# Distances inside the experts' groups, and an alignment that runs in two column halves

## The chip, the cores and the metric

The kernel runs on one core of a Trainium2 chip. The metric is device time in microseconds (us), the median of several runs. The core has five engines that run their own instruction streams and wait for each other by semaphores: PE (TensorE, matmuls), DVE (VectorE), ACT (ScalarE), POOL (GpSimd) and SP (SyncE, which issues the DMAs here).

## What is computed

Sixty-four sequences of 128 tokens, 256 wide, go through four residual steps. Cut to its core the reference is:

```python
x = x + xattn(ctx, layernorm(x), ...)            # attention, 16 heads
x = x + moe_ffn(layernorm(x), ...)               # 16 experts, 4 chosen, and a shared one
x = x + align(ctx, layernorm(x))                 # below
x = x + bit_ffn(layernorm(x), w1, conv, w2)      # ternary weights, depthwise convolution

def align_one(small, large):                     # small = ctx[b], large = layernorm(x)[b]
    aa = sum(small * small, -1)[:, None]; bb = sum(large * large, -1)[None, :]
    D = sqrt(maximum(aa + bb - 2.0 * small @ large.T, 0.0))
    # R[i,j] = D[i,j] + min(R[i-1,j], R[i,j-1], R[i-1,j-1]), then the path is traced back
    # from the corner, and small[i] is added to row j for each (i, j) on the path
```

## The kernel before

The program is a row of stages, each in a block of its own with a barrier at its end: `attention`, `experts`, `distances`, `align`, `conv_ffn`. `x_all` holds all tokens in SBUF throughout. Within a stage every engine has a program written out by hand; the order in it is the order of execution, and semaphores carry the dependences.

`attention` works on pairs of sequences. `norm_a`, `norm_b`, `norm_c` on DVE measure mean and variance of the tokens and of the context and normalise them.

`experts` works on 16 groups of four sequences (GB = 4, NG = 16). A group has per = 12 tiles t = 0 to 11 of hidden units: four shared, then eight routed (TILES = 8). For tile n = 12 g + t, PE does `up_gate(n)` (L838) and then `down_proj(n - 2)` (L876); ACT takes the silu (`gate_silu`, L937) and the high part (`high_hidden`, L943); DVE does `weigh_hidden(n)` (L1067 and L1072), POOL the low part (`low_hidden`, L1120). The next group's input is made in the same loop: DVE normalises at t = 1, PE turns it at t = 5 and 6 (`turn`, L815) and makes the router's scores at t = 7 (L824), and DVE chooses the experts in five steps at t = 8, 9, 10, 11 and 0 (`route_groups` ends at L1032, `route_mask` at L1040, then `route_compare`, `route_rank`, `route_weights`). PE turns the weights at t = 1 (L831), they go by DRAM (`shares`), and SP loads them spread over partitions into `spread`, one slot for each of the eight routed tiles.

`distances` makes D for groups of four sequences in a stage of its own. It loads `ctx` and its transposed copy `ctxT`, measures and normalises x a third time (DVE L1259, L1262, L1271; POOL L1312, L1313), turns it (PE L1197), multiplies it by -2 (`copy_x`, DVE L1281), squares it (ACT L1229), sums the context's squares (ACT L1237), multiplies (PE L1212 with a matrix of ones, L1214 with `ctxT`), adds and clamps (DVE L1290), takes the root (ACT L1246) and stores to `dist` in DRAM.

`align` loads `dist` to SBUF with 64 sequences on half of the partitions: even rows of D on partitions 0 to 63, odd ones on 64 to 127. DVE makes one row after another: a minimum of the row above with itself shifted (L1533), then a scan along the 128 columns (L1534). So each instruction works on 64 partitions. Each 16 rows (a chunk), `compare` writes flags (L1503, L1504), PE swaps them between the halves (L1445, L1448), `trace` makes a start column for every cell (L1511 and the scan L1517), PE and ACT turn that to `rise` (L1459, L1460, L1475). Then 128 dependent steps trace the path back (L1548). ACT and PE also make the ternary weights of the last stage in here (`sum_up` L1382, `make_ternary` L1393 to L1396).

Of the kernel before, what the change touches and what calls it, by code (L numbers as in the profile page):

```python
# [14 lines left out]
P = 128  # L15
# [8 lines left out]
EPS = 1e-5  # L24
# [47 lines left out]
def attention(nc, dve_step, pool_step, x_all, ident, half, x, ctx, wq, wkv, wo, ln_cols):  # L72
# [16 lines left out]
    with Stage(nc, "attention") as st:  # L89
# [7 lines left out]
        mv = [st.sb(f"mean_var{i}", [P, 4, 2]) for i in range(2)]  # L97
        var_eps = [st.sb(f"var_eps{i}", [P, 4]) for i in range(2)]
# [393 lines left out]
        def dve_program(dve):  # L492
# [196 lines left out]
def experts(nc, dve_step, pool_step, x_all, ident, half, router, bias, gate, up, down, s_gate, s_up, s_down, shares):  # L689
    TILES = ROUTED // P  # L690
    STILES = SHARED // P
    STAGES = 3
    with Stage(nc, "experts") as st:
# [14 lines left out]
        spread = st.sb("spread", [P, TILES, GB * TOK])  # L708
        stage = [spread[:, TILES - 2 * i - 2:TILES - 2 * i, :].rearrange("p m t -> p (m t)") for i in range(STAGES)]
        combT = st.sb("combine_turned", [EXPERTS, GB * TOK])  # L710
# [17 lines left out]
        wsum = st.sb("weight_sum", [P, 2, GB])  # L728
        misc = st.bank("misc")
        g_ps = [st.bank(f"gate{i}") for i in range(2)]  # L730
# [10 lines left out]
        spread_loaded = [st.sem(f"spread_loaded{m}") for m in range(TILES)]  # L741
# [3 lines left out]
        down_made, out_added = st.sems("down_made", "out_added")  # L745

# [34 lines left out]

        def is_routed(n):
            return n % per >= STILES

        def sp_program(sp):
            sp.dma_start(router_w[:, :, :], router.rearrange("(k p) n -> p k n", p=P)).then_inc(small_loaded, 16)
            sp.dma_start(bias_w[:, :], bias).then_inc(small_loaded, 16)
            for n, (src, buf, hi, lo) in enumerate(staged):
                if n >= STAGES:
                    sp.wait_ge(w_split, n - STAGES + 1)  # L790
                sp.dma_start(buf, src).then_inc(stage_loaded[n % STAGES], 16)
            for g in range(NG):
# [3 lines left out]
                for m in range(TILES):  # L796
                    if g:
                        sp.wait_ge(silu_weighed, TILES * (g - 1) + m + 1)
                    elif m == TILES - 2 * STAGES:
                        sp.wait_ge(w_split, R_DOWN)  # L800
                    for e in range(2):
                        sp.dma_start(spread[e * HID:(e + 1) * HID, m, :],
                                     shares[g % 2, 2 * m + e:2 * m + e + 1, :].broadcast_to([HID, GB * TOK])
                                     ).then_inc(spread_loaded[m], 16)

        def pe_program(pe):
# [74 lines left out]

            for k in range(KD):
                turn(0, k)
            route_scores(0)
            for n in range(N + 2):
                g, t = divmod(n, per)
                if n < N:
# [5 lines left out]
                if g + 1 < NG:  # L893
                    if t in (5, 6):
                        turn(g + 1, t - 5)
                    if t == 7:
                        route_scores(g + 1)

        def act_program(act):
# [5 lines left out]
            def copy_x(g, k):  # L905
                act.wait_ge(turned, 2 * g + k + 1)
                if g and not k:
                    act.wait_ge(logits_made, g)
                    act.wait_ge(xT_split, g)
                act.copy(xT[:, k, :], misc[:, :]).then_inc(xT_copied, 1)  # L910
# [15 lines left out]
            def copy_weights(g):  # L926
                act.wait_ge(comb_turned, g + 1)
                if g:
                    act.wait_ge(shares_stored, 16 * g)
                act.copy(combT[:, :], misc[0:EXPERTS, :]).then_inc(comb_ready, 1)  # L930
# [38 lines left out]
        def dve_program(dve):  # L969
# [11 lines left out]
            def norm(g):  # L981
# [6 lines left out]
                if g:  # L988
                    dve.wait_ge(turned, 2 * g)
                dve.wait_ge(rstd_made, g + 1)  # L990
# [70 lines left out]
            def weigh_hidden(n):  # L1061
                s = n % 2
                dve.wait_ge(silu_made, n + 1)
                if is_routed(n):
                    g, m = divmod(spreads(n), TILES)
                    dve.wait_ge(spread_loaded[m], 32 * (g + 1))
# [7 lines left out]
            def add_out(g):  # L1074
# [4 lines left out]
                made.then_inc(out_added, 1)  # L1079

# [7 lines left out]
            for n in range(N + 2):  # L1088
# [10 lines left out]
                if n >= 8 and (n - 8) % per < 5 and (n - 8) // per + 1 < NG:  # L1099
                    route[(n - 8) % per]((n - 8) // per + 1)  # L1100

        def pool_program(pool):
# [19 lines left out]

            inverse_std(0)
            low_x(0)
            for n in range(N):
                g, t = divmod(n, per)
                low_hidden(n)
                if g + 1 < NG:
# [4 lines left out]

        with nc.Block() as block:
            block.sync(sp_program)
            block.tensor(pe_program)
            block.scalar(act_program)
            block.vector(dve_program)
            block.gpsimd(pool_program)

def distances(nc, dve_step, pool_step, x_all, ident, half, ctx, ctxT, dist):
    with Stage(nc, "distance") as st:
# [1057 lines left out]
```

## Time and profile before

| | us |
|---|---|
| median of 3 runs | 3542.32 (3541.22 to 3543.53) |
| the profiled execution | 3543.53 |
| its span in the trace | 3541.8 |
| attention, until | 1841 |
| experts, until | 2739.7 |
| distances, until | 2837 |
| align, until | 3057 |
| conv_ffn, until | 3541.8 |

PE is busy 89% of the span, DVE 69%, ACT 52%, POOL 38%. These are means over stages with different limits, so they are read by stage: a windows view gives for a stretch how long each engine was busy, and which clock TensorE was granted (1.00 is 2.4 GHz, 0.50 is 1.2 GHz). A timeline view gives single instructions with start and duration; "[2.65 <-DVE ...]" behind one is how long its engine had been idle and what ended that.

### The profile page before, as it was taken

What the parts mean: (1) busy time and instruction counts of PE and PEld (TensorE: products, weight loads), DVE (VectorE), ACT (ScalarE), POOL (GpSimd) and SP (SyncE); (2) the same over time, 40 slices, a digit from 0 to 9 for tenths busy, and PEclk for the clock granted to TensorE, in tenths of its full rate; (3) what the DMA queues carried; (4) which work ended last, traced back from release to release, by engine and by line L of the source; (5) the groups of instructions that cost most, each with busy time, mean ns of one, the idle gap of its engine ahead of it and who ended that gap; (6) DMA issues with size and microseconds to landing.
All of it is one profiled execution on the core that took longest, in us unless ns stands there. A gap on an engine that the chain in (4) does not pass through costs nothing. (4 is left out here: it accounts for less than half of the span.)

```text
span 3541.8 us, 63842 instructions
## 1 busy us (share of the span) xinstructions
PE 3136.5 (89%) x23236; PEld 2706.4 (76%) x23236; DVE 2437.3 (69%) x5376; ACT 1838.3 (52%) x4701; POOL 1345.0 (38%) x1112
## 2 busy tenths in 40 slices
PE   7999999999999999999978999999999811177876
PEld 6888888888888888888877888888888800155655
DVE  6666666666666666666646656566564989689997
ACT  5565565555556555555633333333332602299996
POOL 2333333333333333333322333333333200078887
PEclk9999999999999999999989999999999955598888
DMA  4000000000000000000011011110111740001100
GB/s 152 5 7 7 5 7 5 7 7 4 8 4 7 4 7 8 4 7 4 5 37 59 33 49 32 42 49 25 49 49 35 225 86 0 12 31 37 42 30 31
DMA packets 104181, 107.96 MB, mean 30 GB/s; under 512 B 7872, under 2 KB 85184, under 8 KB 103872
## 3 DMA queue, kind: packets, MB, share of 16 engines
q1 hardware_dynamic: 103872, 103.88, 9.9%
q8 instruction: 189, 3.10, 0.4%
q14 instruction: 120, 0.98, 0.1%
HBM read 90.75 MB, written 13.11 MB: 29 GB/s over the span
## 5 line engine op out<-in xcount | busy, mean ns | idle before, releaser
L671 POOL TENSOR_TENSOR attention_prob<-attention_prob,attention_inv_sums 128x1024 f32<-128x1024 f32 x256 | 479.6, 1894 | 410.1 <-DVE attention_inv_sums L565 410.1
L442 ACT ACTIVATE attention_prob<-attention_turns,attention_neg_max 128x256 f32<-128x256 f32 x1024 | 468.7, 483 | 174.6 <-DVE attention_neg_max L556 174.6
L1120 POOL TENSOR_TENSOR experts_hidden_lo<-experts_weighed,experts_hidden_hi 128x512 fp32r<-128x512 f32 x192 | 251.8, 1312 | 552.2 <-ACT experts_hidden_hi L943 552.2
L572 DVE COPY attention_probT<-attention_turns 128x512 f32<-128x512 f32 x512 | 329.1, 685 | 169.2 <-PE attention_turns L329 169.1
L556 DVE TENSOR_REDUCE attention_neg_max<-attention_turns 128x2 f32<-128x512 f32 x512 | 318.1, 684 | 45.3 <-PE attention_turns L319 44.4
L943 ACT ACTIVATE experts_hidden_hi<-experts_weighed 128x512 fp32r<-128x512 f32 x192 | 121.4, 632 | 423.6 <-DVE experts_weighed L1072 423.6
L433 ACT COPY attention_v<-attention_turns 128x512 f32<-128x512 f32 x256 | 151.0, 590 | 316.5 <-PE attention_turns L263 316.5
L329 PEld LDWEIGHTS attention_turns<-ident,attention_prob 128*128 128x128 f32 x2048 | 240.2, 141 | 39.7 <-POOL attention_prob L671 4.2
L329 PE MATMUL attention_turns<-ident,attention_prob 128*128 128x128 f32 x2048 | 266.1, 273 | 3.7 <-POOL attention_prob L671 3.7
L1067 DVE TENSOR_TENSOR experts_silu<-experts_silu,experts_spread 128x512 f32<-128x512 f32 x128 | 89.3, 698 | 260.6 <-ACT experts_silu L937 259.5
L345 PE MATMUL attention_heads_out<-attention_probT,attention_v 128*64 128x128 f32 x4096 | 253.7, 277 | 0.8 <-DVE attention_probT L572 0.8
L345 PEld LDWEIGHTS attention_heads_out<-attention_probT,attention_v 128*64 128x64 f32 x4096 | 222.7, 137 | 18.2 <-DVE attention_probT L572 1.2
L660 POOL TENSOR_TENSOR attention_kv_lo<-attention_kv_full,attention_kv_hi 128x256 fp32r<-128x256 f32 x124 | 90.4, 729 | 375.0 <-ACT attention_kv_hi L411 375.0
L565 DVE RECIPROCAL attention_inv_sums<-attention_row_sums 128x4 f32<-128x4 f32 x256 | 44.8, 175 | 268.1 <-ACT attention_prob L442 268.1
L442 ACT ACTIVATION_READ_ACCUMULATOR attention_prob<-attention_turns,attention_neg_max 128x1 f32 x1024 | 220.5, 215 | 0.0
L407 ACT ACTIVATE attention_kv_full<-attention_turns,attention_ln_cols 128x128 f32<-128x128 f32 x256 | 102.3, 449 | 225.8 <-PE attention_turns L256 225.8
L876 PE MATMUL experts_out<-experts_down_hi,experts_hidden_hi 128*128 128x256 f32 x768 | 217.6, 283 | 0.4 <-POOL experts_hidden_lo L1120 0.4
L876 PE MATMUL experts_out<-experts_down_hi,experts_hidden_lo 128*128 128x256 f32 x768 | 217.2, 283 | 0.0
L876 PE MATMUL experts_out<-experts_down_lo,experts_hidden_hi 128*128 128x256 f32 x768 | 216.9, 282 | 0.0
L263 PE MATMUL attention_turns<-attention_wkv_hi,attention_kv_hi 128*128 128x512 f32 x512 | 213.6, 417 | 2.1 <-DVE attention_kv_lo L590 2.1
L295 PE MATMUL attention_turns<-attention_kv_hi,attention_wkv_hi 128*128 128x512 f32 x512 | 214.7, 419 | 0.0
L538 DVE SCALAR_TENSOR_TENSOR attention_k_lo<-attention_turns,attention_k_hi 128x512 fp32r<-128x512 f32 x256 | 177.1, 692 | 47.3 <-ACT attention_k_hi L425 41.3
(266 smaller groups left out, 9823.2 us busy)
## 6 DMA issues: line engine op xcount, KB each, us to landing
experts_spread<-shares SPq DMA_DIRECT2D x256, 128.0 KB, 3.0
attention_ctx<-in_ctx SPq DMA_DIRECT2D x32, 256.0 KB, 2.7
distance_ctx<-in_ctx SPq DMA_DIRECT2D x16, 512.0 KB, 4.4
distance_ctxT<-in_ctxT SPq DMA_DIRECT2D x32, 256.0 KB, 5.0
weights_ctx<-in_ctx SPq DMA_DIRECT2D x16, 512.0 KB, 4.0
out<-conv_x_out SPq DMA_DIRECT2D x15, 512.0 KB, 3.0
x_all<-in_x SPq DMA_DIRECT2D x7, 1024.0 KB, 9.3
dist<-distance_dist SPq DMA_DIRECT2D x16, 256.0 KB, 2.4
```

Source lines behind the costliest of these rows:

```text
L263: made = pe.matmul(out, left[l](k), right[r](k), start=n == 0, stop=n == 3 * KD - 1)
L295: made = pe.matmul(bank[:, :].rearrange("p (e c t) -> p c e t", e=2, c=2), wkv_p[l][:, k, w:w + P], (kv_hi, kv_lo)[r][p % 2][:, k, :, :, : ...
L329: made = pe.transpose(bank[:, (2 * h + t) * P:(2 * h + t + 1) * P], prob[n % 2][:, 2 * g + h, t * P:(t + 1) * P], ident[:, :])
L345: made = pe.matmul(heads_out[o * HEAD:(o + 1) * HEAD, (QT * e + m) * TOK:(QT * e + m + 1) * TOK], v[:, home, e, t, h, :], probT[e][:, h, t ...
L433: act.copy(v[:, 0:2 + pj % 2:1 + pj % 2, e, t, :, :].rearrange("p q h c -> p q (h c)"), bank_of("v", c)[:, :].rearrange("p (q c) -> p q c" ...
L442: made = act.activation(prob[n % 2][:, h, :], bank_of("s", 2 * n + e)[:, m * 256:(m + 1) * 256], ACT.Exp, bias=neg_max[:, n % 2, 2 * e + m ...
L538: return dve.scalar_tensor_tensor(lo, view, scale, hi.bitcast(F32), ALU.mult, ALU.subtract)
L556: made = dve.tensor_reduce(neg_max[:, n % 2, 2 * e:2 * e + 2], bank_of("s", 2 * n + e)[:, :].rearrange("p (h c) -> p h c", h=2), AX.X, ALU ...
L572: dve.tensor_copy(probT[n % 2][:, 2 * g:2 * g + 2].rearrange("p h t c -> p (h t c)"), bank_of("t", 2 * n + g)[:, :]).then_inc(p_copied, 1)
L671: pool.tensor_tensor(prob[n % 2][:, :, :], prob[n % 2][:, :, :], inv[:, n % 2, :].unsqueeze(2).broadcast_to([P, QH, 2 * TOK]), ALU.mult).t ...
L876: made = pe.matmul(out_ps[i // 2][:, (i % 2) * DIM:(i % 2 + 1) * DIM], l[n % 3][:, i * TOK:(i + 1) * TOK], down_w[r][:, m, :], start=t == ...
L1120: pool.tensor_tensor(hid_lo[n % 3][:, :], weighed[n % 2], hid_hi[n % 3][:, :].bitcast(F32), ALU.subtract).then_inc(hid_split, 1)
```

## The change

The stage `distances` is gone. What it did is spread over the program:

- In `attention`, `norm_c` gets two more DVE instructions for each pair of sequences, each on 128x2 numbers: from mean and variance they make the context's sum of squares in `ctx_norm`.
- In `experts`, the distances of group g are made while group g + 1 is worked on ("far"). DVE measures at t = 2, normalises at t = 7, copies the turned halves times -2 at t = 8 and 9, clamps at t = 11. POOL makes the inverse deviation at t = 2 and, at t = 9, squares both halves (L1261 twice) and adds them (L1266). PE turns one half at t = 8 and one at t = 9 (L931), both ahead of that tile's `up_gate`, and multiplies at t = 11 ahead of `up_gate` (L942 with a matrix of 0.25, L944 twice, for each of four sequences: 12 matmuls where there were 16). The last group follows behind the loop. The squared distance is stored, without the root.
- `spread` has six slots in place of eight, used as a ring, and the tile `far` shares its first partitions with the weights on their way to DRAM.
- In `align`, D is cut by columns: partitions 0 to 63 have columns 0 to 63 of all rows, partitions 64 to 127 have columns 64 to 127, two rows behind (LAG = 2). One DVE instruction makes row t of the left half and row t - 2 of the right half, 128 partitions by 64 or 65 columns, in 130 steps in place of 128. D is loaded in four parts of 8, 24, 32 and 64 rows, each in two DMAs, in pieces of 64 numbers (256 bytes) where a piece was a row of 512 bytes. ACT carries the left half's last number of each row to the right half (`hand_over`), and takes the roots of eight rows at a time (`root`). PE gathers both flags of a chunk by 16 matmuls in place of 4, ACT copies one of them. The ternary weights are made in single ACT steps between the rows. The trace back is as it was.

The core of the diff:

```diff
@@ attention, norm_c
+                mean, var = mv[0][:, 2:4, 0], mv[0][:, 2:4, 1]
+                dve_step(dve, dve.scalar_tensor_tensor(mean_part[:, :], mean, float(DIM), mean, ALU.mult, ALU.mult))
+                dve.scalar_tensor_tensor(ctx_norm[:, 2 * p:2 * p + 2], var, float(DIM), mean_part[:, :], ALU.mult,
+                                         ALU.add)
@@ experts, PE
+            def turn_far(g, k):
+                pe.wait_ge(far_normed, g + 1)
+                if k:
+                    pe.wait_ge(far_copied, 2 * g + 1)
...
+            def multiply(g):
+                pe.wait_ge(ctx_loaded, 32 * (g + 1))
+                pe.wait_ge(far_copied, 2 * g + 2)
+                pe.wait_ge(far_summed, g + 1)
...
                 g, t = divmod(n, per)
+                for k in range(KD):
+                    if far_in(n, 8 + k) is not None:
+                        turn_far(far_in(n, 8 + k), k)
+                if far_in(n, 11) is not None:
+                    multiply(far_in(n, 11))
                 if n < N:
                     up_gate(n)
@@ experts, DVE, at the end of a tile's work
+                if far_in(n, 2) is not None:
+                    measure_far(far_in(n, 2))
+                if far_in(n, 7) is not None:
+                    norm_far(far_in(n, 7))
+                for k in range(KD):
+                    if far_in(n, 8 + k) is not None:
+                        copy_far(far_in(n, 8 + k), k)
+                if far_in(n, 11) is not None:
+                    clamp(far_in(n, 11))
@@ align, loads
-            rows = dist.rearrange("b (s h) j -> b s h j", h=2)
-            for c in range(LOADS):
+            for c, (a, b) in enumerate(LOADS):
                 for h in range(2):
-                    sp.dma_start(cost[lanes[h], 1 + c * LR:1 + (c + 1) * LR, 1:], rows[:, c * LR:(c + 1) * LR, h, :]
+                    sp.dma_start(cost[lanes[h], 1 + h * LAG + a:1 + h * LAG + b, 1:], dist[:, a:b, h * W:(h + 1) * W]
@@ align, ACT
+            root(0)
+            for t in range(N):
+                hand_over(t)
+                if t % PIECE == 3:
+                    root(t // PIECE + 1)
```

What this moves, at the places of which the next sections speak. On DVE in `experts`, from the last two instructions of `route_groups` (t = 8) to the weighing of tile 9. Before:

```order
L1031 TENSOR_TENSOR experts_tops<-experts_tops 128x16
L1032 TENSOR_TENSOR experts_group_score<-experts_tops 128x16
L1067 TENSOR_TENSOR experts_silu1<-experts_silu1,experts_spread 128x512
L1072 TENSOR_TENSOR experts_weighed<-experts_silu1,experts_up1 128x512
L1000 TENSOR_TENSOR experts_group_compare<-experts_group_score 128x16
```

After (`experts_far_ps` is the PSUM bank that holds the turned half):

```order
L1111 TENSOR_TENSOR experts_tops<-experts_tops 128x16
L1112 TENSOR_TENSOR experts_group_score<-experts_tops 128x16
L1187 TENSOR_SCALAR experts_xT<-experts_far_ps 128x512
L1147 TENSOR_TENSOR experts_silu1<-experts_silu1,experts_spread 128x512
L1152 TENSOR_TENSOR experts_weighed<-experts_silu1,experts_up1 128x512
L1080 TENSOR_TENSOR experts_group_compare<-experts_group_score 128x16
```

The copy L1187 of the first turned half stands behind the whole of `route_groups`; the second stands in the same way behind `route_mask`, a tile later.

On POOL, around t = 9 of a group, after (before, the five `experts_hidden_lo` rows follow each other directly):

```order
L1249 TENSOR_TENSOR experts_hidden_lo0<-experts_weighed,experts_hidden_hi0 128x512 [waits experts_hidden_high]
L1261 TENSOR_TENSOR experts_xn<-experts_xT 128x512 [waits experts_far_copied,experts_far_turned]
L1261 TENSOR_TENSOR experts_xn<-experts_xT 128x512 [waits experts_far_copied]
L1266 TENSOR_TENSOR experts_far<-experts_xn 128x512 [waits experts_shares_stored,experts_far_stored,experts_far_squared]
L1249 TENSOR_TENSOR experts_hidden_lo1<-experts_weighed,experts_hidden_hi1 128x512 [waits experts_hidden_high]
```

Three more instructions stand between the low parts of tiles 9 and 10, and PE's `multiply` waits for the last of them.

## Rows read from the trace of the kernel before

**Rows 1.** Windows: us, busy time and count by engine, then clock, DMA share, GB/s.

```profile
1936.00:2740.00 804.00, 799.51 (x4692) 701.66 (x4689) 489.16 (x1157) 254.74 (x428) 285.55 (x222) 1.00 0.13 41
2739.70:2837.00 97.30, 78.68 (x640) 75.25 (x640) 83.72 (x289) 60.96 (x177) 20.46 (x34) 0.93 0.76 217
```

**Rows 2.** Timeline, PE, first matmul of `up_gate` at t = 5 and 7.

```profile
2111.03 0.39 PE L838 MATMUL experts_gate<-experts_xT_hi,experts_gate_hi 128*128 128x512 f32 x1
...
2120.23 0.48 PE L838 MATMUL experts_gate<-experts_xT_hi,experts_gate_hi 128*128 128x512 f32 x1
```

**Rows 3.** Timeline, PE, first matmul of `up_gate` at t = 9 and 11.

```profile
2130.54 0.40 PE L838 MATMUL experts_gate<-experts_xT_hi,experts_gate_hi 128*128 128x512 f32 x1
...
2138.99 0.39 PE L838 MATMUL experts_gate<-experts_xT_hi,experts_gate_hi 128*128 128x512 f32 x1
```

**Rows 4.** Timeline, DVE: last instruction of `route_groups` (t = 8), of `route_mask` (t = 9).

```profile
2132.47 0.17 DVE L1032 TENSOR_TENSOR experts_group_score<-experts_tops 128x16 f32<-128x16 f32 x1
...
2137.76 0.22 DVE L1040 TENSOR_TENSOR experts_masked<-experts_masked,experts_group_neg 128x64 f32<-128x64 f32 x1
```

**Rows 5.** Timeline, POOL, the low part of tile 9.

```profile
2135.02 1.31 POOL L1120 TENSOR_TENSOR experts_hidden_lo<-experts_weighed,experts_hidden_hi 128x512 fp32r<-128x512 f32 x1 [2.92 <-ACT experts_hidden_hi L943]
```

**Rows 6.** Lines by form, DVE in `distances`: count, busy us, mean ns, idle before.

```profile
L1281 DVE TENSOR_SCALAR distance_xT<-distance_turned 128x512 f32<-128x512 f32 x32 | 20.4, 679 | 0.0
...
L1290 DVE TENSOR_SCALAR distance_squared_dist<-distance_dist_ps,distance_ctx_norm 128x128 f32<-128x128 f32 x64 | 17.6, 338 | 7.2 <-PE distance_dist_ps L1214 7.2
```

**Rows 7.** Timeline of `distances`: DVE's first normalising, and two matmul groups on PE.

```profile
2743.32 1.38 DVE L1271 TENSOR_SCALAR distance_xn<-x_all,distance_mean_var,distance_rstd 128x256 f32<-128x256 f32 x4 [1.47 <-POOL distance_rstd L1313]
...
2757.61 0.61 PE L1212 MATMUL distance_dist_ps<-distance_xT_square,distance_ones 128*128 128x128 f32 x4
...
2758.50 0.61 PE L1212 MATMUL distance_dist_ps<-distance_xT_square,distance_ones 128*128 128x128 f32 x4
```

**Rows 8.** Timeline, PE in `conv_ffn`: what follows a wait of 2 to 3 us.

```profile
3112.67 0.63 PE L1732 MATMUL conv_hidden_turned<-ident,conv_act_h 128*128 128x128 f32 x4 [2.65 <-DVE conv_h_absmax_part L2005]
...
3141.63 0.63 PE L1732 MATMUL conv_hidden_turned<-ident,conv_act_h 128*128 128x128 f32 x4 [1.97 <-DVE conv_h_absmax_part L2005]
...
3499.36 0.96 PE L1732 MATMUL conv_hidden_turned<-ident,conv_act_h 128*128 128x128 f32 x4 [2.46 <-DVE conv_h_absmax_part L2005]
```

**Rows 9.** Windows, columns as in rows 1: after the first of these waits.

```profile
3113.90:3117.30 3.40, 3.40 (x12) 2.71 (x11) 2.77 (x8) 3.40 (x9) 1.09 (x1) 0.51 0.00 0
```

**Rows 10.** Lines by form, DVE, columns as in rows 6.

```profile
L1534 DVE TENSOR_TENSOR_SCAN align_cost<-align_best,align_cost 64x128 f32<-64x128 f32 x128 | 53.6, 419 | 12.0 <-DMA align_cost<-dist 7.6
...
L1533 DVE TENSOR_TENSOR align_best<-align_cost 64x128 f32<-64x128 f32 x127 | 36.3, 286 | 4.3
...
L1517 DVE TENSOR_TENSOR_SCAN align_back<-align_left,align_moved 128x1024 bf16<-128x1024 bf16 x8 | 18.3, 2292 | 0.3
...
L1504 DVE TENSOR_TENSOR align_left<-align_cost,align_best 128x1024 bf16<-128x1024 f32 x8 | 9.7, 1218 | 0.0
...
L1052 DVE TENSOR_TENSOR experts_combine<-experts_score,experts_rank 128x64 f32<-128x64 f32 x2 | 0.5, 226 | 0.1
```

**Rows 11.** Windows: while `dist` is loaded, and while `ctx` and weights are.

```profile
2840.00:2845.00 5.00, 0.00 (x0) 0.00 (x0) 0.00 (x0) 0.00 (x0) 0.00 (x0) 0.50 1.24 190
...
2862.00:2865.00 3.00, 0.00 (x0) 0.00 (x0) 2.76 (x8) 0.00 (x0) 0.00 (x0) 0.50 1.04 380
```

**Rows 12.** Timeline: SP's loads of `dist`, DVE's first row, its last `trace`.

```profile
2836.96 16.24 SPq L1434 DMA_DIRECT2D align_cost<-dist  x8
...
2845.20 0.42 DVE L1534 TENSOR_TENSOR_SCAN align_cost<-align_best,align_cost 64x128 f32<-64x128 f32 x1 [7.56 <-DMA align_cost<-dist]
...
2990.75 2.29 DVE L1517 TENSOR_TENSOR_SCAN align_back<-align_left,align_moved 128x1024 bf16<-128x1024 bf16 x1
```

More of the change, by code:

```diff
@@ L780, in spreads, with far_in @@
             return g * TILES + max(0, t - STILES)
+        def far_in(n, tile):
+            g, t = divmod(n, per)
+            return g - 1 if t == tile and 0 < g < NG else None
         def is_routed(n):
@@ L897, in pe_program @@
                         route_scores(g + 1)
+            for k in range(KD):
+                turn_far(NG - 1, k)
+            multiply(NG - 1)
         def act_program(act):
@@ L1100, in dve_program @@
                     route[(n - 8) % per]((n - 8) // per + 1)
+                if far_in(n, 2) is not None:
+                    measure_far(far_in(n, 2))
+                if far_in(n, 7) is not None:
+                    norm_far(far_in(n, 7))
+                for k in range(KD):
+                    if far_in(n, 8 + k) is not None:
+                        copy_far(far_in(n, 8 + k), k)
+                if far_in(n, 11) is not None:
+                    clamp(far_in(n, 11))
+            measure_far(NG - 1)
+            norm_far(NG - 1)
+            for k in range(KD):
+                copy_far(NG - 1, k)
+            clamp(NG - 1)
         def pool_program(pool):
@@ L1377, in means, with sum_up @@
         dve.reciprocal(self.inv[:, :], self.mean[:, :]).then_inc(self.inverted, 1)
[L1379 to L1387 removed]
+    def sum_up(self, act, n):
+        if not n:
+            act.wait_ge(self.loaded, 96)
+        made = act.activation(self.junk[:, :], self.raw[:, n, :], ACT.Abs, accum_out=self.sums[:, n:n + 1])
+        if n:
+            made.then_inc(self.summed, 1)
+        else:
+            self.act_step(act, made)
@@ L1479, in act_program, with hand_over, root @@
-            for c in range(CHUNKS):
-                rises(c)
-                if c == 2:
-                    weights.sum_up(act)
-                if c == 5:
-                    weights.make_ternary(act, 0)
-                if c == 6:
-                    weights.make_ternary(act, 1)
+            def hand_over(t):
+                act.wait_ge(row_made, t + 1)
+                act.copy(best[lanes[1], place(t + LAG), 0:1], cost[lanes[0], t + 1, W:W + 1]).then_inc(handed, 1)
+            def root(p):
+                for c, (a, b) in enumerate(LOADS):
+                    if PIECE * p == a:
+                        act.wait_ge(loaded[c], 32)
+                a = 1 + PIECE * p
+                b = min(a + PIECE, SLOTS)
+                if not p:
+                    act.activation(cost[lanes[0], a:b, 1:], cost[lanes[0], a:b, 1:], ACT.Sqrt)
+                    made = act.activation(cost[lanes[1], a + LAG:b, 1:], cost[lanes[1], a + LAG:b, 1:], ACT.Sqrt)
+                elif PIECE * p < N:
+                    made = act.activation(cost[:, a:b, 1:], cost[:, a:b, 1:], ACT.Sqrt)
+                else:
+                    made = act.activation(cost[lanes[1], a:b, 1:], cost[lanes[1], a:b, 1:], ACT.Sqrt)
+                made.then_inc(rooted, 1)
@@ L1488, in pool_program @@
+            rises(CHUNKS - 2, 0)
+            for b in range(2):
+                copy_left(CHUNKS - 1, b)
+            for b in reversed(range(2)):
+                rises(CHUNKS - 1, b)
         def pool_program(pool):
```

505 lines of the change are left out of this document (240 added, 265 removed).

## The prediction, made before the changed kernel ran

> **What bounds the kernel now.** I read the windows by stage first, then the timeline of each engine over one group of `experts`, then the stages `distances` and `align`. In `experts` PE is busy 799.51 of 804.00 us at clock 1.00, DVE 489 and POOL 286 [rows 1]: every instruction that PE gets here, and every wait, lengthens the program, while DVE and POOL have room on the mean. `distances` lasts 97.3 us with no engine full [rows 1]. In `align` DVE is a chain of dependent instructions on 64 partitions: from its first row at 2845.20 to the end of the last `trace` scan at 2990.75 + 2.29 = 2993.04 are 147.8 us [rows 12].
>
> **The stage that goes.** −97.3 us. Its last group stays, behind the loop, as a chain with nothing beside it. In the old stage the first normalising begins 3.6 us after the start at 2739.70 and takes 1.4 us [rows 1, 7]. Then come two turns and two copies (1.1 us each at the lower clock, an estimate from twice the rate in rows 2, and 0.68 us [rows 6]), 3.6; POOL's second square and its sum, 2 x 1.31 [rows 5], 2.8 with the handovers; the multiplication, which at clock 1.00 costs 0.89 us for 8 matmul records [rows 7], so 2.7 us for 24 (12 fp32 matmuls, two records each) and 5.4 us at the lower clock; the clamps, 4 x 0.29 = 1.2 (mean 0.338, overlapping [rows 6]); a store and the barrier, 3 us. Together 21 us (bounds 16 and 26). Net **−76**.
>
> **PE's new work in a group.** From the `up_gate` of t = 5 to that of t = 7 are 9.20 us with two turns between [rows 2], from t = 9 to t = 11 8.45 us without [rows 3]: 0.75 for two turns. Multiplying costs 2.7 us and 0.1 for the switch. Together 3.5 us, nothing hides it. PE idles 4.5 us in all 15 groups [rows 1], mostly where it waits for the combine weights; that goes: −0.3. So **+3.2** a group.
>
> **The first new wait.** PE's turn of the second half stands ahead of `up_gate` at t = 9 and waits for `copy_far(g, 0)`, since both halves use one bank. That copy stands on DVE behind all of `route_groups`, which ends at 2132.47 + 0.17 = 2132.64 [rows 4]. With the copy (0.06 + 0.68 us [rows 6]) it is done at 2133.40, while PE is through with t = 8 at 2130.54 [rows 3]. Both sides shift alike with the turn at t = 8. PE waits **2.9 us**, and all of PE's queue with it.
>
> **The second.** `multiply` stands ahead of `up_gate` at t = 11 and waits for POOL's sum. The chain from t = 9: `route_mask` ends at 2137.76 + 0.22 = 2137.98 [rows 4], `copy_far(g, 1)` at 2138.72, the second square (1.31 [rows 5]; the first is done by then) and the sum at 2141.5 with 0.1 for each handover. PE is there at 2138.99 [rows 3]. PE waits **2.6 us**. The two waits add up, because everything between them hangs on PE's own results. DVE's clamp (1.2 us at t = 11) delays the routing weights by less than PE has been delayed (6 to 9 us), so it costs nothing; if PE did not wait, it would cost at most that 1.2 us.
>
> Sum: 3.2 + 2.9 + 2.6 = 8.7 us in each of 14 groups, 122 us. In the last one nothing is routed: 3.5 us of work, and waits of 0.2 and 1.3 us by the same reckoning without the routing steps, 5 us. **+127**. `measure_far` and `norm_far` (1.8 and 1.4 us at t = 2 and 7) fall where DVE has time; POOL's three instructions at t = 9 (3.9 us) delay the low part of tile 10, which PE wants two tiles later; SP's store and two loads stand between its loads of `spread`, in a stage with a DMA share of 0.13 [rows 1]. At nothing, with 0 to 15 us as the bound if the store (aliased with the weights' tile) comes late by up to 1 us a group.
>
> **TensorE's clock.** Each wait also puts the clock at stake. In `conv_ffn` a wait of 2.65 us was followed by 3.4 us at 0.51, and one of 2.46 us by slow transposes (0.96 against 0.63 us); after one of 1.97 us they were fast [rows 8, 9]. 3.4 us at half clock cost PE 1.7 us of work. The wait of 2.9 us is longer than those that were punished; that of 2.6 us is beside them, but PE has been full before it, which it is not in `conv_ffn`. I take one fall a group: 14 x 1.7 = **+24**; bounds are none, 0, and a fall of twice that length after both, 14 x 6.6 = 92.
>
> **Alignment.** A row now is a minimum of 64 columns and a scan of 65. The minimum: 286 ns at 128 columns, 226 ns for a 128x64 instruction of the same kind [rows 10]. The scan: 419 ns at 128 columns, 2292 ns at 1024 [rows 10], so 2.09 ns a column and 288 ns at 65 (bounds 250 and 350). With the same 70 ns of handovers as now, 0.584 us in place of 0.775; 130 steps are 75.9 where 128 were 99.2: −23.3. The chunks cost DVE the same: three instructions of 1.22 and a scan of 2.29 [rows 10] against two, one more and the same scan; 0. Against that:
> - At the end the last `trace` waits for 16 matmuls at the lower clock, a quarter the size of 1024 columns in 4: estimated 3.8 us (2 to 5).
> - ACT carries one number to the right half for each row. DVE has 0.88 us between a row's end and the scan that needs it, and the copy costs some 0.23 with 0.17 of handovers, so it hides, also behind one root or copy of 0.6 us; the 2 us steps of the weights stand where DVE is in `compare` or `trace` (3.7 and 2.3 us). I take +0.7; if ACT is late each time, 10 x 1.2 = 12.
> - The loads. 512-byte pieces arrive at 190 GB/s, larger ones at 380 [rows 11]: 2.7 and at least 2.7 ns a piece, so pieces and not bytes set the rate. 256-byte pieces then need 44 us for the 4.2 MB. The second part (rows 8 to 31) is there 13.8 us after the start, its first root at 14.5. DVE begins at 7.9 (loads, a table load, two roots; 8.2 now [rows 12]), is at row 6 at 11.4 and must wait there, since ACT, which waits for the load inside `root(1)`, carries nothing: +3.4, and +1.3 when ACT waits in the same way for the weights, queued behind D. Bounds 0 and 10.
>
> −0.3 − 23.3 + 3.8 + 0.7 + 4.7 = **−14.4** (−24 to 0).
>
> By the Trainium skill, "DMA: Bandwidth & Descriptors", section "Why small descriptors are slow (HBM only)", a packet has a fixed cost of some three cycles, 11 for 256 bytes, so that halving it would cost little: D would be there in an estimated 26 us and the 3.4 us would go. The same page's "Specifications" put the line rate at 512 bytes and more. Rows 11 speak for a price per piece.
>
> **Attention.** 64 DVE instructions, 0.2 us each, before `add_out`, which waits for PE there: 0 (bound 3).
>
> **Sum**, on the profiled execution's 3543.5 us: −76 + 127 + 24 − 14.4 + 0 = +60.6, 3604.1. That execution is 1.2 us above the median: **3603**.
>
> **Rivals.**
> - *The clock never falls.* The waits stand, PE's full stretches carry the clock over them. 3603 − 24 = 3579.
> - *The clock falls after both waits, for long.* 3603 + 68 = 3671; with the short fall after both, 3627.
> - *Faster: the waits don't come.* The mechanism is that DVE runs ahead in t = 8 and 9, or PE's matmuls in `up_gate` end later by the records than I read them, so that both copies are ready when PE is. The first wait is gone from the point where `route_groups` ends 0.8 us (the copy) before PE is through with t = 8, at 2129.8, which is 2.9 us earlier than its 2132.64 now [rows 3, 4]. Then `experts` gains only 3.2 x 14 + 3.5 + 1.2 x 2 = 51 us, and the sum is −76 + 51 − 14 = −39: 3503. The order on DVE speaks against it.
> - *The alignment gives nothing*, by late carrying or loads: 3603 + 14 = 3617.
> - *The work does not leave the path at all* is what the first sum says already; the opposite, that moved work hides, needs PE to have room, and it has 4.5 us of 804.
>
> **Chances.** Forecast with one fall, or some, a group (3590 to 3648): 0.50. No fall: 0.22. Long falls: 0.10. Alignment nothing beside the forecast: 0.05, within its range. Waits absent or so small that the kernel is faster: 0.13. The range takes in the no-fall case with a gain of 24 in the alignment and a tail of 16, 3579 − 10 − 5 = 3564, and short falls after both with the alignment's gain lost and half of the store's bound, 3627 + 14 + 7 = 3648; outside are the faster case and most of the long falls. A measurement of this kernel tells about 0.2% (7 us) from no change; faster 0.13, same 0.03, slower 0.84.
>
> **What would show it.** In the changed profile: a group of `experts` takes 63 us or more, not 54; PE's L931 of the second half waits some 2.9 us for DVE's L1187, its L942 some 2.6 us for POOL's L1266; the granted clock of the stage is below 1.00; the tail between the last add and `align` is 21 us; a row of `align` 0.58 us with one halt of 3 us near row 6. If PE's waits there are below 1 us, the prediction is wrong by its largest term; if the clock is 1.00, by its third.

## The result

The changed kernel takes 3646.9 us (median of 4 runs, 3645.7 to 3650.5) against 3542.1 before (4 runs): a ratio of 1.0297, 95% interval 1.0279 to 1.0315, so 105 us slower. 3603 was predicted, with a range of 3564 to 3648: the direction and the mechanism held, the size was 44 us short.

The traces of the two profiled executions are split here at the same events: the last add of `attention`, the end of the last add of `experts`, the first load of `align`, the end of the trace back.

| | before, us | after, us | difference | predicted |
|---|---|---|---|---|
| attention, to its last add | 1840.9 | 1848.4 | +7.5 | 0 |
| experts | 898.8 | 1100.3 | +201.5 | +151 |
| distances; after: the last group's | 97.3 | 20.1 | −77.2 | −76 |
| align | 219.1 | 194.7 | −24.4 | −14.4 |
| the rest | 485.7 | 485.1 | −0.6 | 0 |
| span | 3541.8 | 3648.6 | +106.8 | +60.6 |

Windows of the changed kernel: one over the same stretch of `experts` as [rows 1], then two right behind PE's two new waits in one group. The columns are those of [rows 1].

```profile
1936.00:2740.00 804.00, 727.91 (x4126) 643.65 (x4125) 501.96 (x1178) 208.52 (x347) 292.89 (x240) 0.94 0.14 43
2793.92:2797.32 3.40, 3.40 (x11) 2.90 (x12) 0.00 (x0) 0.00 (x0) 0.00 (x0) 0.56 0.00 0
2807.86:2812.86 5.00, 5.00 (x23) 5.00 (x24) 3.22 (x7) 0.00 (x0) 1.26 (x1) 0.50 0.00 0
```

In the same 804 us PE is busy 728 us where it was busy 799.5 [rows 1], and its granted clock is 0.94 where it was 1.00. Behind the two waits of this group it is 0.56 and 0.50, at or near the 1.2 GHz level. Over the 14 groups of this execution it falls behind the first wait in 11 and behind the second in 14. The waits themselves, in the view of waits of `experts` (us in total, times, longest), and two stores of `dist`, one group apart:

```profile
PE experts_far_ps L942 <- POOL experts_far L1266: 53.8, 16, 3.6
PE experts_far_ps L931 <- DVE experts_xT L1187: 40.2, 15, 3.1
...
2822.84 0.37 SPq L822 DMA_DIRECT2D dist<-experts_far  x1
...
2891.11 0.37 SPq L822 DMA_DIRECT2D dist<-experts_far  x1
```

Between these two stores a group takes 68.3 us, where it took 54.1; the 14 groups take 951.3 us together, 68.0 each, because the groups in which the first wait left the clock alone are 1.0 to 2.6 us shorter. These are the two waits that were forecast, on the lines that were forecast. In one group they read so on PE, with the instructions of the first chain on DVE and of the second on DVE and POOL:

```profile
2789.80 0.69 DVE L1152 TENSOR_TENSOR experts_weighed<-experts_silu,experts_up 128x512 f32<-128x512 f32 x1
...
2792.88 0.17 DVE L1112 TENSOR_TENSOR experts_group_score<-experts_tops 128x16 f32<-128x16 f32 x1
2793.09 0.69 DVE L1187 TENSOR_SCALAR experts_xT<-experts_far_ps 128x512 f32<-128x512 f32 x1
...
2793.92 1.09 PE L931 MATMUL experts_far_ps<-ident,experts_xn 128*128 128x128 f32 x4 [2.78 <-DVE experts_xT L1187]
...
2800.22 2.39 DVE L1086 TENSOR_TENSOR experts_group_compare<-experts_group_compare,experts_below 128x16 f32<-128x16 f32 x4
2800.24 1.30 POOL L1249 TENSOR_TENSOR experts_hidden_lo<-experts_weighed,experts_hidden_hi 128x512 fp32r<-128x512 f32 x1 [7.72 <-ACT experts_hidden_hi L1021]
...
2801.51 1.06 POOL L1261 TENSOR_TENSOR experts_xn<-experts_xT 128x512 f32<-128x512 f32 x1
...
2804.09 0.69 DVE L1187 TENSOR_SCALAR experts_xT<-experts_far_ps 128x512 f32<-128x512 f32 x1
...
2804.86 1.42 POOL L1261 TENSOR_TENSOR experts_xn<-experts_xT 128x512 f32<-128x512 f32 x1 [2.28 <-DVE experts_xT L1187]
2806.35 1.36 POOL L1266 TENSOR_TENSOR experts_far<-experts_xn 128x512 f32<-128x512 f32 x1
...
2807.86 0.77 PE L942 MATMUL experts_far_ps<-experts_far,experts_quarters 128*128 128x128 f32 x2 [3.51 <-POOL experts_far L1266]
```

From start to start of `up_gate`, tile by tile, this group loses against the one before the change: 0.5 us at t = 7 to 8 (a turn), 3.7 at t = 8 to 9 (wait 2.8, turn 0.9), 1.1 at t = 9 to 10 (nothing but the lower clock), 8.8 at t = 10 to 11 (wait 3.5, multiplication 5.3) and 0.5 behind it (clock); 0.4 is won at the combine weights. Together 14.2.

### The profile page after: what moved, and what is told of

It reads as the page before. It is cut to its first block and busy times, and to the rows that moved or that the text cites. A ratio compares the mean times of both kernels' runs of the same rounds, so it can differ in the third digit from the quotient of the medians.

```text
span 3648.6 us, 64032 instructions
## 1 busy us (share of the span) xinstructions
PE 3193.5 (88%) x23204; PEld 2757.7 (76%) x23204; DVE 2461.4 (67%) x5446; ACT 1823.0 (50%) x4687; POOL 1405.7 (39%) x1164
## 5 line engine op out<-in xcount | busy, mean ns | idle before, releaser
L1015 ACT ACTIVATE experts_silu<-experts_gate 128x512 f32<-128x512 f32 x192 | 114.2, 595 | 351.4 <-PE experts_gate L879 351.4
```

## Experiments: the two waits and the clock

Theory A: PE pays for its new work, for two waits, and for the half clock behind them. The rivals are that the clock falls for another reason, and that a wait taken away turns up elsewhere. Three kernels form a square with the change: both waits, one, the other, none. A fourth keeps both but leaves PE almost no idle time.

**Both waits away.** On DVE the copies go ahead of the routing step; on POOL the first square goes ahead of the low part of tile 9.

```diff
+                for k in range(KD):
+                    if far_in(n, 8 + k) is not None:
+                        copy_far(far_in(n, 8 + k), k)
                 if n >= 8 and (n - 8) % per < 5 and (n - 8) // per + 1 < NG:
                     route[(n - 8) % per]((n - 8) // per + 1)
...
-                for k in range(KD):
-                    if far_in(n, 8 + k) is not None:
-                        copy_far(far_in(n, 8 + k), k)
...
+                if far_in(n, 9) is not None:
+                    square_far(far_in(n, 9), 0)
                 low_hidden(n)
```

> The changed kernel with one move on DVE: at t = 8 and 9 the copy of the turned half stands ahead of the routing step, not behind it; on POOL the square of the first half stands ahead of the low part of tile 9. Theory A (PE lost 2.8 and 3.5 us a group to two waits, and 4.3 us to the half clock behind them): both waits fall below 0.5 us, the clock of the stage is 1.00, a group takes 57.7 us instead of 68.3, the kernel 3647 - 14 x 10.6 = 3499 us. Theory B (the waits go but the clock still falls, since something else than the waits makes it fall): 3647 - 14 x 6.3 = 3559. Theory C (the copies ahead of the routing make the routing weights late, the waits only move): 3620 to 3650.

Measured: 3527.8 us, 119 less than the change and 15 less than the kernel before (0.9963, 0.9950 to 0.9975). Waits and windows of `experts`:

```profile
PE experts_misc L872 <- DVE experts_combine L1136: 14.2, 14, 1.0
...
PE experts_far_ps L942 <- POOL experts_far L1268: 4.8, 6, 3.6
...
1950.00:2800.00 850.00, 831.03 (x4988) 730.29 (x4987) 607.70 (x1397) 248.04 (x417) 345.55 (x286) 1.00 0.17 51
```

Both waits are gone (3.6 of the 4.8 us are the last group's, behind the loop) and the clock is 1.00. B, that the clock falls without the waits, is excluded. A small part of C is true: PE now waits 1.0 us in each of 14 groups for the combine weights, which DVE makes later, with the clamp ahead of them. Most groups take 59.0 to 59.3 us, not 57.7, and the change's took 68.0 on the mean, not 68.3; by these two the kernel is at 3528 and not at the 3499 that A gave.

**Only the first wait away.**

```diff
+                if far_in(n, 8) is not None:
+                    copy_far(far_in(n, 8), 0)
                 if n >= 8 and (n - 8) % per < 5 and (n - 8) // per + 1 < NG:
...
-                for k in range(KD):
-                    if far_in(n, 8 + k) is not None:
-                        copy_far(far_in(n, 8 + k), k)
+                if far_in(n, 9) is not None:
+                    copy_far(far_in(n, 9), 1)
```

> The changed kernel, only the copy of the first half (t = 8) moved ahead of the routing step; the second stays behind it. Theory A: the first wait (2.8 us) and its half clock (0.4 us in the turn, 1.1 us in up_gate) go, the second wait of 3.5 us stays because its chain starts at tile 9's own results: 3647 - 14 x 4.3 = 3587 us. Theory D (the two waits hang on one chain on DVE, so that what the first gives the second takes): the second wait grows to 6 us, 3647.

Measured: 3574.0 us. The second wait stays at 3.5 us, so D, that it grows by what the first gives, is excluded; but 73 us are won, not 60. The wait, and windows at its end, in two groups:

```profile
2487.24 0.76 PE L942 MATMUL experts_far_ps<-experts_far,experts_quarters 128*128 128x128 f32 x2 [3.48 <-POOL experts_far L1267]
...
2613.80:2618.80 5.00, 5.00 (x34) 4.59 (x35) 3.23 (x7) 0.60 (x1) 1.27 (x1) 1.00 0.00 0
2486.90:2491.90 5.00, 4.66 (x22) 4.69 (x23) 3.56 (x7) 0.00 (x0) 1.60 (x2) 0.50 0.00 0
```

The same wait, after the same work, is followed by the full clock in one group and by half in another. In one such window for each group, behind its wait, the clock is below 1.00 in 5 of 14 groups here (the text recorded for the next run has 4 of 13; by these windows it is 5 of 14); in the change, where the first wait comes two tiles earlier, in 14 of 14.

**Only the second wait away.** On POOL the first square goes ahead of the low part of tile 9, as in `e1_copies_first`; on DVE:

```diff
+                if far_in(n, 9) is not None:
+                    copy_far(far_in(n, 9), 1)
                 if n >= 8 and (n - 8) % per < 5 and (n - 8) // per + 1 < NG:
                     route[(n - 8) % per]((n - 8) // per + 1)
...
+                if far_in(n, 8) is not None:
+                    copy_far(far_in(n, 8), 0)
```

> The fourth corner of a square with the change (both waits), e2_first_copy (second wait only) and e1_copies_first (none): the copy of the second half stands ahead of route_mask, that of the first half behind route_groups, so that PE keeps only the first wait of 2.8 us. If the clock falls after this wait in most groups, as in the change: 3528 + 14 x (2.8 + 1.5) = 3588 us. If it falls after one wait alone in few groups, as after the 3.5 us wait of e2_first_copy (4 of 13): 3528 + 14 x 2.8 + 4 x 1.5 = 3573.

Measured: 3576.5 us. The first wait is there in 14 groups, 2.8 us each (3.1 in two). PE also waits 1.0 us a group for the combine weights, as in `e1_copies_first`. Behind the first wait the clock falls in 8 of 14; in the two shown here it does and does not:

```profile
2732.41 0.63 PE L931 MATMUL experts_far_ps<-ident,experts_xn 128*128 128x128 f32 x4 [2.78 <-DVE experts_xT L1187]
...
2669.49:2672.89 3.40, 3.40 (x11) 2.87 (x12) 0.00 (x0) 0.00 (x0) 1.04 (x1) 0.55 0.01 2
2732.40:2735.80 3.40, 3.39 (x18) 2.87 (x19) 0.69 (x1) 0.60 (x1) 1.04 (x1) 1.00 0.00 0
```

The square is: none 3527.8, first alone 3576.5 (+49), second alone 3574.0 (+46), both 3646.9 (+119). Both together cost 24 us more than the sum, and the clock's windows say where: behind a first wait the second never keeps the full clock, so the change has 25 falls where the two kernels with one wait have 8 and 5. (The waits for the combine weights, 1.0 us in the first two of these four and none in the others, cancel in this comparison.) In the change the second wait lost the clock also in the three groups in which the first had not. What decides in which group a single wait costs the clock, no run here shows.

**Waits kept, idle time filled.** PE runs matmuls that no one reads, ahead of both waits.

```diff
+            FILL = (11, 14)
+
+            def fill(g, count):
+                if g < NG - 2:
+                    pe.wait_ge(tanh_made, g + 3)
+                    for i in range(count):
+                        pe.matmul(misc[:, :], gate_w[0][:, 0, 0:P], xT_hi[g % 2][:, 0, :], start=True, stop=True)
...
                 if k:
+                    fill(g, FILL[0])
                     pe.wait_ge(far_copied, 2 * g + 1)
...
             def multiply(g):
                 pe.wait_ge(ctx_loaded, 32 * (g + 1))
+                fill(g, FILL[1])
```

> The changed kernel, with matmuls that no one reads put into the two waits of PE: 11 of 128x512 ahead of the second turn at t = 9 and 14 ahead of the multiplication at t = 11 (0.23 us each, 2.6 and 3.3 us), in the first 14 of 15 groups. Nothing else changes; the waits' ends stay where they were. Theory A (the clock falls because PE stands idle): granted clock 1.00 in the stage, 3647 - 14 x 4.3 = 3587 us. Theory B (the fp32 multiplication and the turns are slow for another reason): 3647, or up to 10 us more.

Measured: 3596.6 us, 50 less than the change with 350 matmuls more. Windows:

```profile
1950.00:2800.00 850.00, 844.34 (x4954) 735.17 (x4953) 557.08 (x1303) 233.40 (x389) 326.37 (x267) 1.00 0.15 48
```

PE is busy 844 of 850 us, the clock is 1.00, and a group takes 64.0 us where the change takes 68.3. The 14 groups take 896.9 us where the change's profiled execution has 951.3: the half clock cost it 54 us, and by the medians some 50, not the 60 that 14 times 4.3 gives, because the first wait did not cost the clock in every group. The split of the 14.2 us of a group that lost it after both waits is: 4.3 the clock (68.3 less 64.0), 6.3 the waits (2.8 and 3.5), and 3.6 for the rest, which is PE's new work of 4.0 less 0.4 that it waited for the combine weights before. Theory A stands: the same kernel, with the same waits filled, keeps its clock.

## Experiments: attention, which was to cost nothing

With PE busy in all of `attention`, a pair of sequences took 56.26 us before and 56.53 after. Nearly all of it is in `project_q`: its 256-column matmuls start 0.113 us apart before and 0.120 after. First and last of one tile's twelve, before and after:

```profile
1024.49 0.28 PE L263 MATMUL attention_turns<-attention_kv_hi,attention_wq_hi 128*128 128x256 f32 x1
...
1025.74 0.28 PE L263 MATMUL attention_turns<-attention_kv_hi,attention_wq_lo 128*128 128x256 f32 x1
```

```profile
1029.97 0.28 PE L264 MATMUL attention_turns<-attention_kv_hi,attention_wq_hi 128*128 128x256 f32 x1
...
1031.29 0.28 PE L264 MATMUL attention_turns<-attention_kv_hi,attention_wq_lo 128*128 128x256 f32 x1
```

Eleven steps take 1.25 us and 1.32 us. The PE instructions are the same. What differs is where the tiles lie: `mean_part` pushes `kv_hi` and all behind it further from the weights.

```diff
-        mean_part = st.sb("mean_part", [P, 2])
+        mean_part = st.sb("mean_part", [P, 4])[:, 0:2]
```

> The changed kernel, the small tile mean_part in attention given 16 bytes a partition in place of 8, so that all tiles behind it start 8 bytes further; no instruction changes. In attention each 256-column matmul of project_q takes 0.120 us after the change and 0.113 before. Theory L (the start of the tiles in SBUF makes the rate): the rate comes back, 56.54 us a pair become 56.26, the kernel 3647 - 9 = 3638 us. Theory I (the two added DVE instructions cost it): 3647.

The next three leave every instruction of the kernel before as it was and add one tile that nobody uses:

```diff
+        shift = st.sb("shift", [P, 8])
         var_eps = [st.sb(f"var_eps{i}", [P, 4]) for i in range(2)]
```

> The kernel before, with one unused tile of 32 bytes a partition between the small tiles of attention, at the place where the change has mean_part. 
```diff
+        shift = st.sb("shift", [P, 8])
         wq_p = [st.sb(f"wq_{n}", [P, KD, INNER], F32R) for n in ("hi", "lo")]
```

> The kernel before, the same unused 32-byte tile ahead of all tiles of attention, so that the weights' tiles move by 32 bytes as well and their distance to kv_hi stays. No instruction is changed. If the start of the moving operand alone counts: 56.53 us a pair and 3550 us, as in e5_tile_32. If the distance of the two operands counts: 56.26 us a pair and 3542.

Measured: 3541.8 us, 0.9998 (0.9989 to 1.0008), 56.29 us a pair. `kv_hi` starts at the same address as in the run ahead of it and is fast again: not its start alone counts, but how far the two operands lie apart.

```diff
+        shift = st.sb("shift", [P, 32])
         var_eps = [st.sb(f"var_eps{i}", [P, 4]) for i in range(2)]
```

> The kernel before with an unused tile of 128 bytes where e5_tile_32 has one of 32, so that kv_hi is 72,128 bytes behind wq_hi. If the rate repeats every 128 bytes of distance (72,000 fast; 72,032 and 72,064 slow; so 72,128 fast again): 56.26 us a pair, 3542 us. If every other distance is slow: 56.53 and 3550.

Measured: 3536.7 us, 0.9987 (0.9978 to 0.9996), 56.19 us a pair. So, from `wq_hi` to `kv_hi`: 72,000 and 72,128 bytes fast, 72,032 and 72,064 slow. Four distances don't prove a period; they exclude one of 64 bytes (72,000 is fast, 72,064 slow) and agree with one of 128. Why PE's reads should depend on it isn't settled.

## Experiment: the alignment alone

The kernel before, with the change's alignment and a stage `distances` that stores D squared:

```diff
-                act.activation(dt_[s][:, :, :], sq[s][:, :, :], ACT.Sqrt).then_inc(rooted, 1)
...
-                    sp.wait_ge(rooted, g)
-                    sp.dma_start(dist[GB * g - GB:GB * g].rearrange("b i j -> i b j"), dt_[(g - 1) % 2][:, :, :]
+                    sp.wait_ge(clamped, g)
+                    sp.dma_start(dist[GB * g - GB:GB * g].rearrange("b i j -> i b j"), sq[(g - 1) % 2][:, :, :]
```

> The kernel before with only the alignment of the change: the stage distances stays and stores squared distances without its ACT root, align works in two column halves. From the change's trace, where start to end of the trace back are 194.7 us in place of 219.1: 3542 - 24 = 3518 us. Rival (the alignment is fast there only since the distances had long been written): its first row later by some 3 us, 3521. Rival (the prediction's -14): 3528.

Measured: 3515.9 us, 0.9927 (0.9912 to 0.9941). The alignment takes 194.3 us here, the same as in the change: this half of the change was worth 26 us by itself (25 of them inside `align`, 219.1 to 194.3), and the other half lost 131. Its first row comes 5.04 us after the start, as in the change (5.05), so the rival that it profits there from distances written long before is excluded.

## A version that beats both

`e1_copies_first` with the clamp behind the routing weights, the multiplication behind `up_gate`, and a larger `mean_part`:

```diff
-        mean_part = st.sb("mean_part", [P, 2])
+        mean_part = st.sb("mean_part", [P, 16])[:, 0:2]
...
-                if far_in(n, 11) is not None:
-                    multiply(far_in(n, 11))
                 if n < N:
                     up_gate(n)
+                if far_in(n, 11) is not None:
+                    multiply(far_in(n, 11))
...
-                if far_in(n, 11) is not None:
-                    clamp(far_in(n, 11))
+                if t == 0 and g >= 2:
+                    clamp(g - 2)
```

> e1_copies_first with three more edits: mean_part takes 64 bytes, so that kv_hi starts 32 behind a multiple of 64 again; the multiplication stands behind up_gate at t = 11; the clamp stands behind the routing weights at t = 0 of the next group, not ahead of them. Theory: attention 8 us less; PE's wait of 1.03 us a group for the combine weights and of 0.23 for the sum go: 3528 - 8 - 15 x 1.2 = 3502 us. Rival (the weights' copy then waits for the store of far, which the later clamp delays, and the first routed tile for its loads): 3520 or more, with PE waits at t = 4.

Measured: 3513.4 us, 0.9919 (0.9904 to 0.9934). The wait for the combine weights falls from 14.2 to 4.4 us:

```profile
PE experts_misc L872 <- DVE experts_combine L1136: 4.4, 14, 0.5
PE experts_far_ps L942 <- POOL experts_far L1268: 3.6, 1, 3.6
```

A group takes 58.1 us, but attention stayed at 56.53 us a pair. I had taken the start of `kv_hi` for the cause; the distance is 72,064 here, one of the slow ones. The next kernel, against this one:

```diff
-        mean_part = st.sb("mean_part", [P, 16])[:, 0:2]
...
         attT_hi, attT_lo = (st.sb(f"attT_{n}", [P, 2, MO, TOK], F32R) for n in ("hi", "lo"))
+        mean_part = st.sb("mean_part", [P, 2])
```

> e8_best with mean_part allocated as attention's last tile instead of one of 64 bytes among the small ones, so that kv_hi starts 72,000 bytes behind wq_hi, as in the kernel before and in e6_all_32 (72,064 in e8_best, 72,032 in the change and in e5_tile_32). No instruction is changed. Theory D (the distance of the two operands of project_q decides): 56.26 us a pair, attention ends 8 us earlier, 3513 - 8 = 3505 us. Theory I (what is left in e8_best is the two added DVE instructions): 3513.

Measured: 3505.2 us, 0.9895 (0.9879 to 0.9912), 56.25 us a pair, with the two added DVE instructions in it. They cost nothing; the prediction was right on them and blind to their tile.

```diff
+        shift = st.sb("shift", [P, 32])
         var_eps = [st.sb(f"var_eps{i}", [P, 4]) for i in range(2)]
```

> e9_tile_last with the unused 128-byte tile of e10_tile_128 among attention's small tiles; no instruction is changed. e10_tile_128 took 56.19 us a pair where the kernel before takes 56.26 and came out 5 us faster. If that comes from where the tiles lie, it is to be had here too: 3505 - 5 = 3500 us. If it was the chance of where the clock fell in that run: 3505.

Measured: 3503.0 us, 0.9887 (0.9870 to 0.9903), 56.19 us a pair. By the trace the tile wins 0.07 us a pair, 2 us; the two medians don't tell these kernels apart. It is 144 us faster than the change and 39 faster than the kernel before. Most of these 39 us are the alignment's: `e7_align_alone` is at 3515.9 us, so that the moved distances, well placed and with the same attention (56.26 and 56.25 us a pair), win 11 us (3505.2) of the 97.3 that their stage took.

## Why the prediction was right, and where it was short

- **What bounds the kernel**: right. PE's own work costs in full: in `e1_copies_first`, with no wait to speak of, two turns and the multiplication cost 1.15 and 2.84 us. I had 0.75, from the difference of two spacings [rows 2, 3], and 2.8. With 0.4 us won at the combine weights that is 3.6 to 3.7 a group where I had 3.2.
- **The first wait**: 2.78 us measured, 2.9 predicted, from the order on DVE and four rows.
- **The second wait**: 3.5 against 2.6. The chain is the forecast one, but DVE's four small multiplications in `route_mask` take 2.39 us, not 1.54 as in the kernel before, whose row is the first here:

```profile
2135.00 1.54 DVE L1006 TENSOR_TENSOR experts_group_compare<-experts_group_compare,experts_below 128x16 f32<-128x16 f32 x4
...
2633.09 1.36 POOL L1249 TENSOR_TENSOR experts_hidden_lo<-experts_weighed,experts_hidden_hi 128x512 fp32r<-128x512 f32 x1 [3.04 <-ACT experts_hidden_hi L1021]
...
2633.21 1.27 DVE L1080 TENSOR_TENSOR experts_group_compare<-experts_group_score 128x16 f32<-128x16 f32 x1
...
2635.62 1.52 DVE L1086 TENSOR_TENSOR experts_group_compare<-experts_group_compare,experts_below 128x16 f32<-128x16 f32 x4
```

  In the change POOL's first square follows at once on the low part of tile 9, and the multiplications span both (rows above: they end at 2802.61, POOL at 2802.57). With the square moved in `e1_copies_first` (the last three rows) they take 1.52 again, but other small instructions of the same step now take 1.27 and 1.01 us: there the hold-up has moved, and PE no longer waits for it because the copy stands ahead of the step. I had priced the chain's DVE part from the trace without POOL's new load.
- **The clock**: this is the term that was mis-sized, 24 predicted and 54 measured in the profiled execution (951.3 less 896.9 us), some 50 by the medians. "I take one fall a group" failed twice. Both waits were punished, which I had as a rival with 0.10 (the long falls) and in the range (short ones); and I took a fall's price, 1.7 us, from a stretch of 3.4 us. The second fall lies over the multiplication, and costs 2.4 us in it and 0.4 behind it; the first costs 1.4 where it happens. (Two long falls at my own price are 6.8 us, not the 6.6 that I wrote.)
- **The last group's chain**: 20.1 us against 21.
- **The alignment**: −24.4 against −14.4, just past the end of my bounds (−24). The row was right (0.587 us measured, 0.584 predicted), the start was 3.2 us earlier, not 0.3, since the first part is small, and the loads were better than feared. DVE waits 2.3 us before the last `trace`, not 3.8, and 1.4 us in all for the numbers that ACT carries. The halt near row 6 is there, but 1.2 us long, not 3.4:

```profile
2976.80 0.29 DVE L1579 TENSOR_TENSOR_SCAN align_cost<-align_best,align_cost 128x65 f32<-128x65 f32 x1
2977.13 0.23 DVE L1576 TENSOR_TENSOR align_best<-align_cost 128x64 f32<-128x64 f32 x1
2978.59 0.29 DVE L1579 TENSOR_TENSOR_SCAN align_cost<-align_best,align_cost 128x65 f32<-128x65 f32 x1 [1.24 <-ACT align_best L1461]
...
2972.00:2990.00 18.00, 0.18 (x2) 0.21 (x4) 13.51 (x42) 5.73 (x22) 0.00 (x0) 0.50 1.40 163
```

  The last row is a window over the load: 256-byte pieces arrive at 163 GB/s, 1.6 ns each, where 512-byte pieces took 2.7. "Pieces and not bytes set the rate" was wrong; halving a piece costs a seventh of the rate, and the 4.2 MB of D take 26.5 us by the DMA packets of the trace, not 44. That is what the Trainium skill, "DMA: Bandwidth & Descriptors", section "Why small descriptors are slow (HBM only)", would have given (an estimated 26 us): here the trace agrees with the page and not with my reading of two rates at 512 and 1024 bytes.
- **Attention**: 0 against +7.5. The bound of 3 us looked at instructions only.

The misses in sum: clock +30, second wait +13, first wait −2, PE's work +7, last group +2, attention +7.5, tail −1, alignment −10, the rest −1: +46, as the table has it (106.8 less 60.6). Part of the closeness is luck: the alignment's 10 us hid a quarter of the half clock and the longer wait.

## What to carry to other kernels

When work moves into a stage whose bounding engine is full, look first at where its copies stand in the other engines' queues: two copies on DVE and a square on POOL, moved by one step each, were worth 119 us here, more than the 97.3 us of the stage that went. Price waits of TensorE together with the clock behind them, and lay short multiplications where no wait is ahead of them; a second wait soon after a first one is dearer than either alone. After a new tile in SBUF, compare the spacing of matmuls that were not touched.

## What the runs showed that I had not expected

- **A wait's price in clock is not a function of its length.** 2.8 us cost the full clock in 8 of 14 groups and 3.5 us in 5 of 14, in kernels where the other of the two was gone; 3.5 us in 14 of 14 with another wait two tiles ahead. The first of these kernels also has a wait of 1.0 us at t = 1, the second has none, and their POOL orders differ; what makes the difference stays open.
